# An attention stage whose contexts are made transposed, with the values as the stationary operand

## The reference

```python
q = _apply_rope(proj(Wq, bq)); k = _apply_rope(proj(Wk, bk)); v = proj(Wv, bv)     # 16 heads of 64
# blocks of 128 queries, each with its own and the block before of keys: 256 keys
scores = jnp.einsum('bhnqd,bhnkd->bhnqk', qb, kcat) * scale                        # band mask, first block alone
attn = jax.nn.softmax(scores, axis=-1)
ctx = jnp.einsum('bhnqk,bhnkd->bhnqd', attn, vcat)
return merged @ Wo.T + bo
```

## Time and profile before

| | us |
|---|---|
| median of three runs | 1653.96 |
| the profiled execution, its own time | 1662.5 |
| its span | 1660.7 |
| busy in the span: PE / DVE / ACT / POOL | 1497.6 / 1460.0 / 1289.7 / 967.6 |
| steps of the attention (first scores to last, 63 steps) | 19.6 each |

### The profile page before, as it was taken

How to read it: one execution, slowest core, us unless ns; L and a number is a source line. 1 busy time by engine, 2 the same in 40 slices (tenths; PEclk the granted TensorE clock), 3 DMA queues, 4 the chain that set the end, 5 groups by cost and what they waited for, 6 DMA issues and landing times. The chain is left out here.

```text
span 1660.7 us, 46262 instructions
## 1 busy us (share of the span) xinstructions
PE 1497.6 (90%) x16674; PEld 1129.1 (68%) x16674; DVE 1460.0 (88%) x4009; ACT 1289.7 (78%) x2362; POOL 967.6 (58%) x786
## 2 busy tenths in 40 slices
PE   5999978899989999999999898999998989869998
PEld 4888745566666666666666666666666666658887
DVE  5998588899989999999998998999998989957885
ACT  5999567787868787878787887868787877749996
POOL 4665356565656675656666665666675656613443
PEclk8999998999999999999999999999999999979999
DMA  5233247989999989989998989899999798971331
GB/s 206 91 120 105 76 90 128 163 151 179 156 173 167 175 162 171 163 158 180 166 173 153 179 151 179 147 184 163 183 156 170 152 157 145 175 168 61 105 115 75
DMA packets 721530, 247.87 MB, mean 149 GB/s; under 512 B 687381, under 2 KB 706073, under 8 KB 721305
## 3 DMA queue, kind: packets, MB, share of 16 engines
q1 hardware_dynamic: 720600, 244.53, 76.4%
q10 hardware_dynamic: 704, 0.40, 0.1%
HBM read 47.73 MB, written 25.17 MB: 44 GB/s over the span
## 5 line engine op out<-in xcount | busy, mean ns | idle before, releaser
L1449 ACT ACTIVATE at_prob<-at_prob,at_top 128x256 f32<-128x256 f32 (+1 forms) x1024 | 429.0, 490 | 105.3 <-DVE at_top L1248 102.0
L1248 DVE CUSTOM_DVE_ANT_0 at_prob<-banks,at_masks,pre_s_scale 128x256 f32<-128x256 f32 (+1 forms) x1024 | 420.5, 472 | 15.9 <-PE banks L1690 1.8
L1260 DVE TENSOR_TENSOR at_halves<-at_prob,at_halves 128x1024 f16<-128x1024 f32 (+1 forms) x256 | 306.2, 1212 | 0.7 <-ACT at_halves L1458 0.7
L1583 PE MATMUL banks<-at_xt,pre_w_h 128*128 128x512 f16 x1024 | 299.5, 385 | 5.0 <-DVE at_v_l L1322 4.3
L1690 PE MATMUL banks<-at_kt,at_qt 32*128 32x256 f32 (+1 forms) x4096 | 254.9, 385 | 50.4 <-DVE at_top L1248 21.8
L1194 POOL TENSOR_TENSOR at_c_halves<-at_ctx,at_c_halves 128x1024 f16<-128x1024 f32 x64 | 136.6, 2134 | 275.0 <-DVE at_halves L1260 268.9
L1690 PEld LDWEIGHTS banks<-at_kt,at_qt 32*128 32x128 f32 x4096 | 202.9, 188 | 112.3 <-issue 109.6
L1458 ACT ACTIVATE at_halves<-at_prob 128x1024 f16<-128x1024 f32 (+1 forms) x256 | 262.9, 1027 | 6.5
L1643 PE MATMUL banks<-at_v_h,at_pt 128*128 128x65 f16 x1984 | 209.1, 195 | 51.7 <-DMA at_pt<-at_halves 26.7
L1643 PEld LDWEIGHTS banks<-at_v_h,at_pt 128*128 128x128 f16 x1984 | 181.4, 98 | 107.0 <-issue 51.9
L1163 POOL TENSOR_TENSOR at_kt<-at_k_by 128x512 f32<-128x512 f32 x128 | 163.0, 1273 | 97.0 <-DVE at_halves L1260 93.1
(11 more groups left out here) (126 smaller groups left out, 3162.4 us busy)
## 6 DMA issues: line engine op xcount, KB each, us to landing
f_x<-in_x SPq DMA_DIRECT2D x16, 512.0 KB, 4.0
x_after_ffn<-f_x SPq DMA_DIRECT2D x16, 512.0 KB, 2.6
at_x_ln<-x_after_ffn SPq DMA_DIRECT2D x16, 512.0 KB, 4.8
at_x_res<-x_after_ffn SPq DMA_DIRECT2D x64, 128.0 KB, 2.9
x_after_attention<-at_x_res SPq DMA_DIRECT2D x64, 128.0 KB, 2.7
f_x<-x_after_attention SPq DMA_DIRECT2D x16, 512.0 KB, 4.6
out_x<-f_x SPq DMA_DIRECT2D x16, 512.0 KB, 3.0
at_tables<-in_cos SPq DMA_DIRECT2D x16, 256.0 KB, 3.9
```

The costliest lines, as they stand in the source:

```text
L1248: last = nc.vector.tensor_tensor_reduce(out=prob[:, n % 2, h, low:2 * P], in0=s_ps[:, h, n % 2 * 2 * P + low:(n % 2 + 1) * 2 * P], in1=mas ...
L1260: nc.vector.tensor_tensor(parts[:, 1, :, :], prob[:, n % 2, :, keys_from(t, b):2 * P], parts[:, 0, :, :], ALU.subtract).then_inc(p_low, 1)
L1449: last = nc.scalar.activation(at, at, ACT.Exp, bias=top[:, n % 2, h:h + 1], scale=-1.0)
L1583: last = nc.tensor.matmul(pr_ps[:, half, :].rearrange("p (b t) -> p b t", b=SB), w[wp][:, k, at:at + P], xt[:, r, xp, :, k, :], start=n == ...
```

## The change

The operands of `values_product` change places. The values of a head (128 keys x 64) are now the stationary operand, and the turned probabilities (128 keys x 128 queries) are streamed. Two heads share the array: the even one of a pair writes PSUM partitions 0 to 63, the odd one 64 to 127, so that the context comes out with head and channel on its partitions, as `output` needs it. There are 24 matmuls as before, of 128 streamed columns instead of 64 or 65.

The sums no longer come from TensorE. The exponentials write them by ScalarE's accumulator (`accum_out`, 16 in a step). VectorE takes the reciprocals of two blocks at a time (`inverse_sums`). A reciprocal for each query has to lie along the free axis now and be the same on 64 partitions: `spread` makes this with eight float32 matmuls for two blocks (stationary: the reciprocal's column repeated 64 times; streamed: an identity of 128), twice in a step, into bank `o_ps`, which `output` uses too. ScalarE copies the bank to SBUF (`spread_copy`, 128 x 512, twice in a step). `context` is one multiplication. ScalarE and GpSimd write its halves straight to `ct`; `turn_context`, `c_halves` and the DMA go. The values of a superblock's last block go to one of six rotating slots (`valued`), so `carry_values` goes too. The last hunk below is TensorE's `at_step`; ScalarE's has `spread_copy(t - 1, 1)` ahead of `exponentials(t, 1)` and `spread_copy(t, 0)` ahead of `exponentials(t, 3)`.

```diff
         def context(t, b):
                 dve.wait_ge(pv_done, n + 1)
-                src = c_ps[:, 0:GROUP * VE].rearrange("p (h d) -> p h d", d=VE)
-                nc.vector.reciprocal(inv[:, :, :], src[:, :, HD:VE]).then_inc(inv_made, 1)
-                dve.wait_ge(inv_made, n + 1)
+                dve.wait_ge(spread_made, 2 * t + b // 2 + 1)
...
-                nc.vector.tensor_tensor(ctx[:, t % 2, b, :].rearrange("p (h d) -> p h d", d=HD),
-                                        src[:, :, 0:HD], inv[:, :, :].broadcast_to([P, GROUP, HD]),
+                nc.vector.tensor_tensor(ctx[:, t % 2, b, :], c_ps[:, 0:2 * P], inv_t[:, b // 2, b % 2, :],
                                         ALU.mult).then_inc(ctx_made, 1)
+        def inverse_sums(t, duo):
+                dve.wait_ge(p_made, 4 * t + 2 * duo + 2)
+                need(spread_done, 2 * (t - 2) + duo + 1)
+                nc.vector.reciprocal(inv[:, t % 2, 2 * duo:2 * duo + 2, :],
+                                     sums[:, 2 * duo:2 * duo + 2, :]).then_inc(inv_made, 1)
...
-                    last = nc.scalar.activation(at, at, ACT.Exp, bias=top[:, n % 2, h:h + 1], scale=-1.0)
+                    last = nc.scalar.activation(at, at, ACT.Exp, bias=top[:, n % 2, h:h + 1], scale=-1.0,
+                                                accum_out=sums[:, b, h:h + 1])
...
+        def spread_copy(t, duo):
+                act.wait_ge(spread_done, 2 * t + duo + 1)
+                need(ctx_made, 4 * (t - 1) + 2 * duo + 2)
+                nc.scalar.activation(inv_t[:, duo, :, :].rearrange("p b t -> p (b t)"), o_ps[:, :],
+                                     ACT.Copy).then_inc(spread_made, 1)
...
         def values_product(t, b):
-                for h in range(GROUP):
-                    out = c_ps[:, h * VE:h * VE + VE]
+                for a in range(2):
                     for s, at in enumerate(slots):
-                        ph, pl = (turned_p[:, (e * GROUP + h) * len(slots) + s, :] for e in range(2))
-                        nc.tensor.matmul(out, ph, v_h[:, at, h, :], start=s == 0, stop=False)
-                        nc.tensor.matmul(out[:, 0:HD], ph, v_l[:, at, h, :], start=False, stop=False)
-                        last = nc.tensor.matmul(out, pl, v_h[:, at, h, :], start=False, stop=s == len(slots) - 1)
+                        for m, (v, e) in enumerate(((v_h, 0), (v_l, 0), (v_h, 1))):
+                            for h in (2 * a, 2 * a + 1):
+                                last = nc.tensor.matmul(
+                                    c_ps[h % 2 * HD:(h % 2 + 1) * HD, a * P:(a + 1) * P], v[:, at, h, :],
+                                    turned_p[:, (e * GROUP + h) * len(slots) + s, :],
+                                    start=s == 0 and m == 0, stop=s == len(slots) - 1 and m == 2)
                 last.then_inc(pv_done, 1)
+        def spread(t, duo):
+                pe.wait_ge(inv_made, 2 * t + duo + 1)
+                need(spread_made, 2 * t + duo)
+                need(x_made, t - 5 + duo)
+                for b in (2 * duo, 2 * duo + 1):
+                    for h in range(GROUP):
+                        at = (b % 2 * 2 + h // 2) * P
+                        last = nc.tensor.matmul(
+                            o_ps[h % 2 * HD:(h % 2 + 1) * HD, at:at + P],
+                            inv[:, t % 2, b, h:h + 1].broadcast_to([P, HD]), ident[:, :], start=True, stop=True)
+                last.then_inc(spread_done, 1)
         def output(i):
-                pe.wait_ge(ct_in, 16 * (NG * (i // NG) + NG))
+                pe.wait_ge(ct_low, NG * (i // NG) + NG)
+                pe.wait_ge(spread_made, min(2 * (i + SB) + 3, 2 * STEPS))
...
         def at_step(t):
             queries_of(t + 1, 0)
+            spread(t - 1, 1)
             scores(t, 1)
             values_product(t - 1, 2)
             values(t + 1, 0)
+            spread(t, 0)
             values(t + 1, 1)
```

More of the change, by code:

```diff
@@ L1036, in carried, with valued, pair_of, turned_context @@
         return sum(1 for before in range(t + 1) if before // NG % SPB != SPB - 1)
+    def valued(t, b):
+        return 3 * (t % 2) + b if b < SB - 1 else 6 + t % 6
+    def pair_of(t, half):
+        first, second = valued(t, 2 * half), valued(t, 2 * half + 1)
+        return slice(first, second + 1, second - first)
+    def turned_context(t, part):
+        return ct[:, t // NG % 2, t % NG, part, :, :, :].rearrange("p b a t -> p b (a t)")
     def own(t, b):
@@ L1396, in at_step @@
             context(t - 1, 2)
+            inverse_sums(t, 0)
             p_low_of(t, 1)
@@ L1412, in at_step @@
                 x_low_of(S + 2)
+            inverse_sums(t, 1)
             p_low_of(t, 3)
@@ L1465, in v_high_of @@
                 need(pv_done, 4 * t - 4)
-                need(v_carried, carried(t - 2))
-                at = own(t, 2 * half)
-                nc.scalar.activation(v_h[:, at:at + 2, :, 0:HD],
+                at = pair_of(t, half)
+                nc.scalar.activation(v_h[:, at, :, :],
                                      pr_ps[:, half, :].rearrange("p (b h d) -> p b h d", b=2, d=HD),
@@ L1495, in context_high @@
                     act.wait_ge(past.x_made, 2 * past.CHUNKS)
-                need(ct_in, 16 * t)
-                nc.scalar.activation(c_halves[:, 0, :, :], ctx[:, t % 2, :, :], ACT.Copy).then_inc(ct_high, 1)
+                need(o_done, SB * (t // NG - 1))
+                nc.scalar.activation(turned_context(t, HI), ctx[:, t % 2, :, :], ACT.Copy).then_inc(ct_high, 1)
         def key_copy(t):
@@ L1631, in values_product @@
                 pe.wait_ge(v_low[1], t + 1)
-                if b == 0:
-                    need(v_carried, carried(t - 4))
                 need(ctx_made, n)
@@ L1674, in scores @@
                 if t == 0:
-                    pe.wait_ge(made, MADE)
+                    pe.wait_ge(made, MASKS_MADE)
                     pe.wait_ge(past.gated_made, 2 * past.CHUNKS)
@@ L1718, in last_step @@
             values_product(t, 1)
+            spread(t, 1)
+            values_product(t, 2)
             output(t - 4)
-            values_product(t, 2)
             values_product(t, 3)
@@ L1745, in build @@
         attn = attention_stage(nc, stack, x1, x2, placed(ATTENTION, low),
-                               (bank[:, 4:8, :], pairs[0], bank[:, 2, :], bank[:, 3, :]), prepared, ffn1, bv, bo, cos, sin)
+                               (bank[:, 4:8, :], pairs[0], bank[:, 2, :], bank[:, 3, :]), prepared, ffn1, tiles[-1], bv, bo,
+                               cos, sin)
         ffn2 = ffn_stage(nc, stack, "f2", x2, out, tiles, placed(SECOND, low), (pairs[0], pairs[2], pairs[3], pairs[1]),
```

67 lines of the change are left out of this document (28 added, 39 removed).

## The result

The changed kernel takes 1868.06 us (median of four, 1867.05 to 1869.74), the kernel before 1655.32 us (median of four). The ratio is 1.1267, 95% interval 1.1234 to 1.1301: 213 us slower. The forecast was slower, 1782 us, so the direction held and the size did not: 3.3 us a step instead of 2.0.

The account below looks back on a forecast made before the run. TensorE (17.7 us), VectorE and DMA (18.1 each) were all near the 19.3 us step; afterwards TensorE sets it. Terms 0.0 + 1.9 + 0.5 + 0.5 - 0.6 - 0.3 = +2.0 us, 64 steps, +128 us: 1782 us, range 1630 to 1975.

Parts of the forecast that it names:

- Products with the values: TensorE's 24 value matmuls a block: 0.74 us against 0.73, so 0.0 us a step, bounds -0.3 and +2.3.
- The spreads: New float32 matmuls on TensorE, two groups a step at 0.97 us: +1.9 us a step, bounds +1.7 and +3.5.
- Changes of split: TensorE going into or out of the half split about ten times more: +0.5 us a step, bounds 0 and 1.0.
- The new wait: TensorE's `output` waits until ScalarE has copied the spread reciprocals from `o_ps`: +0.5 us a step, bounds 0 and +1.9.
- The accumulators: Sixteen exponentials on ScalarE at 0.1 us each, 1.6 us a step, covered by ScalarE's slack.
- DMA waits: TensorE's waits for turned contexts go altogether, those for turned probabilities mostly: -0.6 of 0.7 us a step.
- Other waits: TensorE's waits on VectorE and GpSimd shrink as these gain slack: -0.3 us a step, bounds 0 and -0.85.
- A: Rival: the DMA queue holds the step and TensorE's new work falls into its holes; 1612 us, chance 0.15.
- D: Rival: gains and costs cancel, the cheap end of the sum; 1654 us, chance 0.07.
- B: Rival: the column halves do not overlap on TensorE, no wait for ScalarE; +5.4 us a step, 2000 us, chance 0.18.
- C: Rival: paired work is cheap but the accumulator dear, so ScalarE sets the step; 1712 us, chance 0.05.
- if TensorE's share falls: Sign against the forecast, which expected TensorE's busy share in the attention at 93% or more.

Follow-up runs that it names:

- early copy: Changed kernel with ScalarE's `spread_copy(t, 0)` moved right behind the third block's exponentials, ahead of their high half and the value copies: 1730.24 us, ratio 1.0456.
- unturned contexts: Kernel before without the turn of the contexts, their halves written straight to where the output product reads them (wrong values): 1614.91 us, ratio 0.9747.
- one half alone: Changed kernel with all 24 value products of a block in column half 0, odd heads left out of the context: 1954.63 us, ratio 1.1781.
- one spread: Changed kernel with each group of eight float32 spreads replaced by one float16 matmul of 512 columns: 1893.68 us, ratio 1.1441.
- without accumulators: Changed kernel with exponentials writing no accumulator and the sums set to one: 1830.45 us, ratio 1.1032.
- later spread: Changed kernel with the first spread behind both value products, its copy behind the third block's high half, ahead of the value copies: 1787.61 us, ratio 1.0773.

## Why the prediction was right in direction and short in size

- **Products with the values**, 0.0 a step (-0.3 to +2.3): right that two halves run side by side. A block takes 0.80 us from start to the next work instead of 0.73; 0.66 of it is streaming (24 times 28 ns), so the loss of 12% that was carried over from the row-split scores is not there and the streaming alone comes to the cheap bound of -0.3. The other 0.14 goes to changes of split.
- **The spreads**, +1.9 on TensorE: right as work, 1.02 us each (710.50 to 711.52) against 0.97, though again as 0.87 of streaming without loss and 0.15 beside it. Wrong as time: taking 1.6 us of it out gave 13 us with the early copy and nothing without it.
- **Changes of split**, +0.5: too low. It is 0.09 us into the half split (706.49 + 0.43 to 707.01; next to nothing behind scores, 711.52 + 1.94 to 713.47), 0.14 more in each of four blocks and 0.15 in each of two groups of spreads, about 1.2 us a step, above the upper bound of 1.0. That these are all changes of split is inferred from what streaming leaves over. The three terms together, -0.3 + 1.7 + 1.2 = 2.6, are near the 2.4 that was added up, because two misses cancel.
- **The new wait**, +0.5 (0 to +1.9): this is the step that failed. It is 1.9 us on average, the dear bound, and there in every step from 400 to 1400 us, plus the half clock that follows some of them; that is 1.4 us more than was taken, 90 us in 64 steps, and accounts for the error of 86. The prediction said that ScalarE "stands ready more often" as TensorE's step grows, because it had 4 us idle. It has 5.9 us idle now and is never ready there, for two reasons. Its idle time lies before the first maxima, at the other end of the loop. And the value copies, which the prediction put ahead of the spread copy, themselves wait for the product right ahead of `output`: however much slack ScalarE has, three copies then stand between that product and `output`. The shortest of the 43 waits is 1.78 us, so the lower bound of 0 could not be had in this order. Moving the copy took 138 us off, more than the whole error.
- **The accumulators**, covered: right in the kernel before (5 us) and with the early copy (6 to 11 us), wrong in the changed kernel (38 us), where twelve of them are in the run that the copy ends, though most of it comes by way of the clock. The prediction has no term for the clock. The size, 0.1 us in the pace, was right: starts lie 0.49 us apart (709.74, 710.23) instead of about 0.40.
- **DMA waits**, -0.6: right, shown by the unturned contexts (41 us). **Other waits**, -0.3: the rows for contexts and queries vanished, but a wait for the reciprocals of 0.5 us a step took their place.
- The rivals: A (faster) and D are excluded by the result. B was wrong in the changed kernel; its price of 2000 us was not tested, as the run with one half alone (1955 us) leaves the spreads paired and keeps the wait that B did without. C's engine lies in the chains, but by the place of one copy and not by the sum of its work, 16.6 us a step.
- The signs: the prediction would be wrong "if TensorE's share falls". It did, in the middle of the attention from 92% to 89%, and that sign fits the step that failed: TensorE's work grew about as forecast, and its idle time grew with it.

What stays open is the rest of 75 us with the early copy. TensorE is busy for 97% there, yet taking 1.6 us of spreads out of each step gives 13 us and taking the accumulators out 6: when TensorE's work shrinks, its waits for the reciprocals, for the spread copy and for the maxima grow. That a second chain lies within some 0.2 us a step of TensorE's own work is inferred from this; which one it is was not tested.

## What to carry to other kernels

A wait that is added in the middle of an engine's program costs what the chain behind it costs, not what the waiting engines' idle shares suggest. Follow the awaited instruction back on its own engine: if the run without a gap starts where the waiting work ends, it is a loop. Then ask of every instruction in the run what it waits for itself: here the value copies wait for the product right ahead of the waiting one, which sets a least wait that no slack removes. Where two such chains are nearly as long, shortening one gives only the difference. Place a copy that another engine waits for ahead of everything on its engine that has slack. Before a DMA is replaced by work on three engines, leave the DMA out once: here that gave 41 us, the most that its removal alone could bring.

## What the runs showed of the hardware

- Matmuls with 64 stationary and 128 streamed columns in float16 run in the two column halves at 28 ns each, whether they alternate singly or in threes, and at 56 ns in one half alone. With 128 stationary and 64 or 65 streamed columns they took 31 ns, so that exchanging the operands gained nothing.
- An accumulator on ScalarE is an instruction of its own, 192 ns long, which adds 0.09 us to the pace (0.49 instead of 0.40).

```profile
L1458 ACT ACTIVATION_READ_ACCUMULATOR at_prob<-at_prob,at_top 128x1 f32 x1024 | 197.1, 192 | 0.0
```

- VectorE's reciprocal of 128 x 256 from PSUM takes 1750 ns, where a multiplication of that size takes 417 to 425; for 128 x 4 it was 176 ns.
- TensorE's clock fell to 1.2 GHz behind some waits before the output product and not behind others. In five kernels (changed, one half alone, one spread, without accumulators, later spread; 400 to 1400 us) none of 151 waits of up to 1.82 us was followed by it, and 39 of the longer ones were. In the kernel before it was also low behind two output products that had waited 0.74 and 0.88 us (at 873.85 and 1030.30), so the length of the one wait does not decide it alone. In the run with one spread TensorE has less work, waits longer and is at the low clock more often, and the kernel is 26 us slower; that the clock is the whole reason was not tested.
